# An embedding, attention and feed-forward stage: its first loads issued at once, and its weight preparation spread over VectorE's order

## The reference, cut to what matters

```python
h = concat([patches @ W + b, table[ids]], axis=1)            # 64 image tokens, 128 text tokens
x = layernorm(h)
scores = (x @ wq.T) @ (x @ wk.T).T / sqrt(256); attn = softmax(causal(scores))
h = h + attn @ (x @ wv.T)
alpha = mean(abs(w)); w_t = sign(w) * (abs(w) > 0.5 * alpha)  # for w_up and w_down
h = h + ternary(gelu(ternary(layernorm(h), w_up)), w_down)
# second layer: log_lam = -8 * softplus(omega) * sigmoid(xi @ Wl.T + bl), and so on
```

## Time and profile before

| | before |
|---|---|
| median of 3 runs | 1068.57 us (1068.31 to 1074.8) |
| profiled execution | 1078.99 us, its span 1077.2 us |
| TensorE (PE) busy in the span | 944.6 us, 88% |
| VectorE (DVE) | 827.7 us, 77% |
| ScalarE (ACT) | 571.5 us, 53% |
| GpSimd (POOL) | 544.5 us, 51% |
| mean granted TensorE clock | 0.947 |

### The profile page before, as it was taken

The page is one execution under the profiler, slowest core; times in us unless marked ns, Lnnn a source line. Parts: engine busy times, 40 slices in busy tenths (PEclk is TensorE's granted clock), DMA queues, the critical chain, the costliest instruction groups (busy, mean ns, idle before and its releaser), DMA issues. The chain is left out here.

```text
span 1077.2 us, 19311 instructions
## 1 busy us (share of the span) xinstructions
PE 944.6 (88%) x5800; PEld 840.2 (78%) x5800; DVE 827.7 (77%) x2441; ACT 571.5 (53%) x1127; POOL 544.5 (51%) x652
## 2 busy tenths in 40 slices
PE   2379999999999999876988999999999999962898
PEld 2269999999999999864567888888888888852787
DVE  2657888888888888764368889989999989874676
ACT  2136555555555555542546666667776667521342
POOL 2126666666666665443424444445555445433463
PEclk9589999999999999987989999999999999965999
DMA  4200311111111114002299999999999999983310
GB/s 140 65 25 26 40 41 40 39 40 44 41 45 39 41 44 156 16 15 73 31 121 130 145 154 150 147 159 153 156 153 151 147 152 137 134 99 102 106 59 20
DMA packets 134814, 96.32 MB, mean 89 GB/s; under 512 B 11208, under 2 KB 129104, under 8 KB 134096
## 3 DMA queue, kind: packets, MB, share of 16 engines
q1 hardware_dynamic: 133200, 91.20, 56.5%
q0 software_dynamic: 1536, 4.20, 1.3%
HBM read 31.92 MB, written 13.11 MB: 42 GB/s over the span
## 5 line engine op out<-in xcount | busy, mean ns | idle before, releaser
L296 POOL TENSOR_TENSOR gelu_lo<-gelu_out,gelu_hi 128x384 fp32r<-128x384 f32 x128 | 151.9, 1206 | 40.5 <-DVE gelu_hi L483 39.4
L893 POOL TENSOR_TENSOR B_decayed_u<-B_scan_in 128x512 f32<-128x512 f32 x48 | 62.0, 1293 | 102.9 <-DMA B_scan_in<-B_stage 92.0
L657 PE MATMUL psA<-ternary_down,gelu_hi 128*128 128x256 f32 x384 | 101.2, 299 | 10.8 <-POOL gelu_lo L296 10.8
L610 PE MATMUL psA<-x2T_hi,ternary_up 128*128 128x384 f32 x256 | 93.7, 366 | 10.6 <-DVE residual L590 10.5
L657 PE MATMUL psA<-ternary_down,gelu_lo 128*128 128x256 f32 x384 | 96.9, 288 | 0.0
L610 PE MATMUL psA<-x2T_lo,ternary_up 128*128 128x384 f32 x256 | 87.5, 342 | 0.0
L657 PEld LDWEIGHTS psA<-ternary_down,gelu_hi 128*128 128x128 f32 x384 | 74.4, 194 | 16.0 <-POOL gelu_lo L296 15.1
L1129 PE MATMUL psB<-Win_hi,B_x_hi 128*128 128x512 f32 x192 | 83.7, 436 | 0.0
L1141 PEld LDWEIGHTS psB<-B_partial_dots,B_minus_same_batch 128*128 128x128 f32 x384 | 66.7, 195 | 19.9 <-DVE B_partial_dots L1025 8.8
L881 POOL TENSOR_TENSOR B_y<-B_scan_in,B_states 128x512 f32<-128x512 f32 x48 | 61.9, 1290 | 38.4 <-ACT B_states L952 38.4
L1041 DVE SCALAR_TENSOR_TENSOR psB<-B_decayed_u,psB 128x128 f32<-128x128 f32 x192 | 68.0, 354 | 13.6 <-PE psB L1141 13.3
(11 more groups left out here) (247 smaller groups left out, 3350.6 us busy)
## 6 DMA issues: line engine op xcount, KB each, us to landing
B_scan_in<-B_stage SPq DMA_DIRECT2D x192, 256.0 KB, 8.3
patches<-in_patches SPq DMA_DIRECT2D x16, 384.0 KB
B_residual<-layer_out SPq DMA_DIRECT2D x48, 128.0 KB, 5.1
out_dram<-B_residual SPq DMA_DIRECT2D x48, 128.0 KB, 5.0
C_raw<-in_experts SPq DMA_DIRECT2D x8, 768.0 KB, 4.2
layer_out<-residual SPq DMA_DIRECT2D x32, 128.0 KB, 1.8
layer_out<-residual SPq DMA_DIRECT2D x32, 64.0 KB, 2.0
weight_stage<-in_upT SPq DMA_DIRECT2D x1, 1024.0 KB, 5.7
```

Of the source, the lines that this page charges most:

```text
L296: nc.gpsimd.tensor_tensor(act_l[:, k, :], act[:, k % DEEP, :], act_h[:, k, :].bitcast(F32), ALU.subtract).then_inc(s["ffn_lo"], 1)
L610: last = nc.tensor.matmul(out, a, b, start=(n == 0), stop=(n == len(terms) - 1))
L657: last = nc.tensor.matmul(ps[:, 6 + k // 2, (k % 2) * D:(k % 2 + 1) * D], x[:, c, k * P:(k + 1) * P], dn_w[:, c, :], start=(c == 0 and x i ...
L893: nc.gpsimd.tensor_tensor(lu[:, j % 2], ring[:, j % R_RING, :, LAM, :], ring[:, j % R_RING, :, U, :], ALU.mult).then_inc(s["lu"], 1)
```

## The change

All of it is in part A. `order` gets the pieces merge, qk_split, abs_up, abs_down, tern_up and tern_down, which do their work for tile 0 alone (offset 1 for those of down, so that they run in period -1, and 2 for the others, period -2); `ternary` and `chunk` 2 leave `prepare`. SyncE issues the loads of period -3 without waits: `weight_stage` holds the three chunks side by side, and the two ternary weights land in `W.raw_l` and `W.raw_v`. The ids and the gather of tile 0 move to period -4. VectorE casts the patches of tile 0 before it splits weights. The merge writes bank 4 and runs after `tok` of tile 0. `up` of tile 0 waits for the up weights alone, `down` for both. The load of the channel vectors moves to period 12, and the softplus and the store of its rows to period 15, where ScalarE loads the Gelu table again behind it.

```diff
+        MERGED = ps[:, 4, :].rearrange("p (a b) -> p a b", a=DC)
...
-        order = """ids_load exp gelu_table tok ternary.0 up.0 up.1 pT patch_split patch_load emb pT_split root1 gelu.0 gelu.1 v
-                v_split apply1 up.2 up.3 gelu.2 add.1 up.4 pv gelu.3 add.2 xT gelu.4 up.5 x_split ternary.1
-                gelu.5 up.6 add.3 up.7 gelu.6 gelu.7 exp_table t h1 root2 gather t_split add.4 add.5
+        order = """ids_load exp gelu_table tok merge up.0 up.1 pT patch_split patch_load emb pT_split root1 gelu.0 gelu.1 v
+                v_split apply1 qk_split abs_up abs_down up.2 up.3 gelu.2 add.1 up.4 pv gelu.3 add.2 xT gelu.4 up.5 x_split
+                gelu.5 up.6 add.3 up.7 gelu.6 gelu.7 exp_table t h1 root2 gather t_split tern_up tern_down add.4 add.5
                 down.0 down.1 score scale2 add.6 add.7 x2T down.2 max ss x2_split rscale
                 h2.0 h2.1 h2.2""".split()
         order = [(w.split(".")[0], int((w + ".0").split(".")[1])) for w in order]
         offset = {"up": 0, "gelu": 0, "add": 0, "down": 0, "ss": 0, "rscale": 0, "h2": 0, "tok": 2, "emb": 2, "root1": 2, "apply1": 2,
-                  "xT": 2, "x_split": 2, "t": 2, "t_split": 2, "score": 2, "max": 2, "ternary": 2, "patch_load": 4, "ids_load": 3,
+                  "xT": 2, "x_split": 2, "t": 2, "t_split": 2, "score": 2, "max": 2, "abs_up": 2, "abs_down": 1, "tern_up": 2, "tern_down": 1, "merge": 2, "qk_split": 2, "patch_load": 4, "ids_load": 3,
                   "patch_split": 3, "gather": 3}
...
-        chunks_of = {-3: (0, 1, 2)}
-        tern_of = {-2: (0, 1)}
+        chunks_of = {-3: (0, 1)}
...
+        stage_at = (0, 1024, 1536)
+        raw_tern = [W.raw_l[:].rearrange("p a b -> p (a b)"), W.raw_v[:].rearrange("p a b -> p (a b)")]
+        tern_in = [s["tern_in0"], s["tern_in1"]]
...
                 if g == -4:
+                    sp.dma_start(ids[:, 0, :], io["ids"][0]).then_inc(ids_in[0], 16)
+                if g == G - 4:
                     sp.dma_start(vec[:], io["vectors"]).then_inc(s["vec_in"], 16)
-                if g == 1:
+                if g == G - 1:
                     sp.wait_ge(s["c8"], 1)
                     sp.dma_start(W.rows[0].rearrange("(k m p) -> p k m", p=P, k=3), vec[:],
                                  allow_slow_non_contiguous=True).then_inc(s["rows_out"], 16)
                 if g == G - 4:
+                    sp.wait_ge(s["w_sum"], 4)
                     for a, b in ((W.raw_in, io["WinT"]), (W.raw_l, io["WlT"]), (W.raw_v, io["WvT"]), (W.raw_out, io["WoutT"])):
                         sp.dma_start(a[:].rearrange("p a b -> p (a b)"), b).then_inc(s["raw_in"], 16)
-                for n in chunks_of.get(g, ()):
-                    src, _, _, cols = chunks[n]
-                    if n >= 2:
-                        sp.wait_ge(s["w_lo"], n - 1)
-                    sp.dma_start(stage_half[n % 2][:, 0:cols], src).then_inc(stage_in[n % 2], 16)
                 if g == -3:
+                    def chunk(n):
+                        src, _, _, cols = chunks[n]
+                        sp.dma_start(stage[:, stage_at[n]:stage_at[n] + cols], src).then_inc(stage_in[n], 16)
+
+                    chunk(0)
+                    chunk(1)
                     sp.dma_start(wq, io["wq"]).then_inc(s["qk_in"], 16)
                     sp.dma_start(wk, io["wk"]).then_inc(s["qk_in"], 16)
                     sp.dma_start(bias_tok[:], io["tokb"]).then_inc(s["const_in"], 16)
-                for n in tern_of.get(g, ()):
-                    sp.wait_ge(s["w_lo"], 3)
-                    wait(sp, s["w_sum"], 2 * n)
-                    sp.dma_start(stage[:], tern[n][0]).then_inc(s["tern_in"], 16)
+                    chunk(2)
+                    for n in range(2):
+                        sp.dma_start(raw_tern[n], tern[n][0]).then_inc(tern_in[n], 16)
...
-                if kind == "ids_load":
+                if kind == "ids_load" and not (isinstance(n, int) and n == 0):
...
+            def gather(n, sl, half):
+                pool.wait_ge(ids_in[sl], 16 * (half + 1))
+                wait(pool, s["h1_done"], n - 1)
+                settle(pool)
+                for j in range(2):
+                    pool.indirect_dma_start(
+                        emb[:, sl, 1 + j, :], None, io["table"],
+                        bass.IndirectOffsetOnAxis(ap=ids[:, sl, j:j + 1], axis=0),
+                    ).then_inc(text_in[sl], 16)
+
+            def prepare(g):
+                if g == -4:
+                    gather(0, 0, 0)
+
...
-                if g == -2:
+                if g == G - 1:
                     sc.wait_ge(s["c1"], 1)
                     nc.scalar.activation(soft[:, 1, :], soft[:, 0, :], ACT.Exp, scale=-1.0).then_inc(s["c2"], 1)
                     sc.wait_ge(s["c3"], 1)
                     nc.scalar.activation(soft[:, 3, :], soft[:, 2, :], ACT.Ln).then_inc(s["c4"], 1)
+                    wait(sc, s["gelu_warmed"], G)
+                    nc.scalar.activation(warm_gelu[:], ones[:, 0:1], ACT.Gelu)
                 for n in chunks_of.get(g, ()):
-                    _, hi_, _, cols = chunks[n]
-                    sc.wait_ge(stage_in[n % 2], 16 * (n // 2 + 1))
-                    nc.scalar.activation(hi_, stage_half[n % 2][:, 0:cols], ACT.Copy).then_inc(s["w_hi"], 1)
-                if g == -3:
-                    sc.wait_ge(s["merge_ps"], 1)
-                    nc.scalar.activation(qk_h[:], SC[:, 0:DC * D].rearrange("p (a b) -> p a b", a=DC), ACT.Copy,
-                                         scale=float(D) ** -0.5).then_inc(s["qk_ready"], 1)
+                    chunk_hi(n)
+
+            def chunk_hi(n):
+                _, hi_, _, cols = chunks[n]
+                sc.wait_ge(stage_in[n], 16)
+                nc.scalar.activation(hi_, stage[:, stage_at[n]:stage_at[n] + cols], ACT.Copy).then_inc(s["w_hi"], 1)
...
+                if kind == "qk_split" and isinstance(n, int) and n == 0:
+                    sc.wait_ge(s["merge_ps"], 1)
+                    nc.scalar.activation(qk_h[:], MERGED, ACT.Copy, scale=float(D) ** -0.5).then_inc(s["qk_ready"], 1)
+                    chunk_hi(2)
...
-            def ternary(n):
-
-                out = tern[n][2]
-                v.wait_ge(s["tern_in"], 16 * (n + 1))
-                nc.vector.tensor_reduce(abparts[:], stage[:].rearrange("p (a b) -> p a b", a=32), AX_X, ALU.add,
+            def abs_sum(n):
+                raw = raw_tern[n]
+                v.wait_ge(tern_in[n], 16)
+                nc.vector.tensor_reduce(abparts[:], raw.rearrange("p (a b) -> p a b", a=32), AX_X, ALU.add,
                                         apply_absolute_value=True).then_inc(s["w_abs_parts"], 1)
                 v.wait_ge(s["w_abs_parts"], n + 1)
                 nc.vector.tensor_reduce(absum[:, n:n + 1], abparts[:], AX_X, ALU.add).then_inc(s["w_abs"], 1)
...
+                raw, out = raw_tern[n], tern[n][2]
...
             def prepare(g):
+                if g == G - 1:
+                    softplus()
+                if g == -3:
+                    patch_hi(0)
+                for n in chunks_of.get(g, ()):
+                    chunk_lo(n)
                 if g == -2:
-                    softplus()
-                for n in chunks_of.get(g, ()):
-                    _, hi_, lo_, cols = chunks[n]
-                    v.wait_ge(s["w_hi"], n + 1)
-                    nc.vector.tensor_tensor(lo_, stage_half[n % 2][:, 0:cols], hi_.bitcast(F32),
-                                            ALU.subtract).then_inc(s["w_lo"], 1)
-                if g == -3:
-                    v.wait_ge(s["qk_ready"], 1)
-                    nc.vector.scalar_tensor_tensor(out=qk_l[:], in0=SC[:, 0:DC * D].rearrange("p (a b) -> p a b", a=DC),
-                                                   scalar=float(D) ** -0.5, in1=qk_h[:].bitcast(F32), op0=ALU.mult,
-                                                   op1=ALU.subtract).then_inc(s["qk_ready"], 1)
                     v.wait_ge(s["const_in"], 16)
                     v.wait_ge(s["mask_ready"], 1)
+
+            def chunk_lo(n):
+                _, hi_, lo_, cols = chunks[n]
+                v.wait_ge(s["w_hi"], n + 1)
+                nc.vector.tensor_tensor(lo_, stage[:, stage_at[n]:stage_at[n] + cols], hi_.bitcast(F32),
+                                        ALU.subtract).then_inc(s["w_lo"], 1)
+
+            def patch_hi(n):
+                v.wait_ge(s["patch_in"], 16 * (n + 1))
+                wait(v, s["tok_done"], n)
+                nc.vector.tensor_copy(pat_h[:], patches[:]).then_inc(s["patch_hi"], 1)
...
+                if kind == "qk_split" and isinstance(n, int) and n == 0:
+                    v.wait_ge(s["qk_ready"], 1)
+                    nc.vector.scalar_tensor_tensor(out=qk_l[:], in0=MERGED, scalar=float(D) ** -0.5,
+                                                   in1=qk_h[:].bitcast(F32), op0=ALU.mult,
+                                                   op1=ALU.subtract).then_inc(s["qk_ready"], 1)
```

(30 more changed lines are left out.)

35 lines of the change are left out of this document (7 added, 28 removed).

## The result

The changed kernel takes 1065.61 us, median of 20 runs (1054.2 to 1069.39); the kernel before takes 1076.15, median of 20 (1068.31 to 1085.06). The ratio is 0.9907, 95% interval 0.9885 to 0.9929. The forecast was 1054.2 in 1048.5 to 1061, so the time lies above the range. Two things must be kept apart. The three runs of before that stood ahead of the prediction (median 1068.57; they are three of the 20) lay low in a spread of 17 us: over 20 runs the median is 7.6 us higher. And the shift itself is 1065.61 - 1076.15 = -10.5 us, not -14.4.

A forecast was written before the change was run, and what follows sets the result against it. TensorE was taken to bound the repeated periods, untouched; the head was to be bound by the second patches' landing at 16.9 us. Head -16.6 plus last period +2.2 gave -14.4, from 1068.57 to 1054.2 us, range 1048.5 to 1061.

The forecast's parts named there:

- Sum: Whole kernel: head -16.6 and last period +2.2 give -14.4 us, taken from the median of 1068.57 to 1054.2.
- Tile 0: Head, cast of second patches to row maxima: cast -18.0 us, `t` -19.5, maxima -19.0 after tern_up's +0.5.
- Tile 0, next period: Head, to up.0: abs_down costs nothing, tern_down delays x_normed 3.9 us, up.0 +2.4, so first period starts -16.6 us.
- I take 390: Head, early loads: 3.67 MB left after 7.4 us move at 390 GB/s in 9.4 us, patches 1 landing at 16.9.
- I give 0 in the sum, and 2 us either way in the range: Head, TensorE's clock: half-clock stretches fall otherwise; 18 `tok` matmuls take 1.9 us at full, 3.8 at half clock.
- Last period: Last tile: softplus before gelu.0, with two table loads, delays it by +2.2 us; bounds 1.6 to 3.9.
- A port, weighed: Head, tern_down beside GpSimd's gather issue: an issue holds VectorE back by next to nothing, despite the skill's shared-port rule.
- (c): Rival, head: shared port makes tern_down wait for both gather issues, +2.1 us, 1056.3; chance 0.10.
- (b): Rival, head: loads at 299 GB/s put the cast at 19.7, +2.8, half-clock `tok` +1.7: 1058.7 us; chance 0.17.
- (a): Rival, head: second patches not held back by the queue, cast at 13, 3.9 us more gain, 1050.3; chance 0.12.
- (d): Rival, repeated periods: head hands over a lasting half clock, about 24 us per whole period, 1078, slower; chance 0.03.
- (e): Rival, head: early loads bring nothing; about 4 us gained against 2.4 and 2.2 of delays, 1068; chance 0.03.

The follow-up runs named there:

- e1: Changed kernel with both 1 MB ternary loads issued behind the patches of tile 1 instead of ahead; 0.9833 of the kernel before.
- e7: Changed kernel with the gather of tile 0 back in its old place, period -3; 0.9899 of the kernel before.
- e3: Changed kernel with tern_up ahead of `t`, abs_down behind t_split, tern_down at the head of the next period; 0.981 of before, second run 1057.95 us.
- e5: Changed kernel with the edits of e1, e2 and e3 together, run twice; 0.9822 and 0.9853 of the kernel before.
- e6: Changed kernel with the edits of e1, e2 and e3 and the filler matmuls of e4; 0.9843 of the kernel before.
- e2: Changed kernel with the softplus, its load and its store back in the head and the Gelu reload gone; 0.9816 of the kernel before.
- f1: Changed kernel with unread matmuls, 12 behind the scores of tile 1 and 8 behind x2T of tile 0; 1064.88 us, single run.
- e4: Changed kernel with filler matmuls that nobody reads in seven places of the head; 0.9873 of the kernel before.

## Why the prediction was wrong

**The base, "Sum".** "The median is 1068.57 ... a shift holds for it: 1054.2" is the step that failed most. I had seen that the profiled execution (1078.99) and the median of three runs lay 1% apart, and took the three for the kernel's time. Over 20 runs it is 1076.15. The mean of the three runs shown differs from it by 5.6 us; with the profiled execution as a fourth sample the spread of 10.7 us was in plain view, and the range should have held half of it on the upper side. With the forecast's own shift and the base of 20 runs the number would have been 1061.8, still 3.9 us below 1065.61; with the means of all runs it is 1060.5 against 1063.0. (The 1064.6 that the forecast names for the profiled execution lies 1 us from the median by luck: its base was 2.8 us too high and its shift 3.9 too large.)

**The shift, "Tile 0" and "Tile 0, next period".** Step by step, forecast against the mean of three profiles of each kernel:

- Cast of the second patches: -18.0, measured -17.05 (18.0 instead of 16.9). The mechanism, the queue that holds a small late load, was right (e1, e7), and so was "I take 390": by 7.4 us the three profiles had moved 1.19 to 1.23 MB (1.18 in the forecast), and from there to 16.5 they ran at 389, 400 and 400 GB/s. The term that was mis-sized is the last one, "so patches 1 land when all 4.85 MB are through": it has the cast follow the bulk of the bytes at once. The first profile (the last column is GB/s):

```profile
7.40:16.50 9.10, 4.71 (x23) 4.63 (x24) 1.83 (x2) 1.58 (x2) 1.66 (x1) 1.00 0.99 389
16.50:18.00 1.50, 0.97 (x5) 0.52 (x3) 0.00 (x0) 0.49 (x1) 0.00 (x0) 1.00 0.17 57
18.00:18.58 0.58, 0.00 (x0) 0.00 (x0) 0.00 (x0) 0.58 (x2) 0.00 (x0) 1.00 0.00 0
```

  The last bytes trickle for 1.5 us, and VectorE starts 0.6 us after the last of them. In the repeats the trickle is 0.4 and 0.9 us, and the start again 0.5 to 0.6 us behind it. The cast so stood 1.0 to 2.1 us behind 16.5.
- Cast to row maxima of tile 0: -1.0, measured -1.26. Its parts came out: xT_lo is held by qk_lo, wv_lo and the sum, 1.1 us (forecast 1.3); `t` no longer waits for a ternary matmul; and from tT_lo to neg_max it takes 6.31 us with tern_up, in all three profiles, 0.5 more than the mean before (6.07, 6.53 and 4.75), as forecast.
- tern_down: "denominators and x_normed end 3.9 us later". ln_den follows tT_lo after 5.16 us instead of 0.87 to 1.45, and the maxima of tile 1 come 2.3 us later.
- Then "`tok` takes 2.2 us more, until about 84.4" and, of the clock, "**I give 0 in the sum, and 2 us either way in the range**": this is the step of the shift that failed. In all seven profiles with tern_down ahead of x_normed and no filler in the pause (1.7 to 3.4 us), `tok` of tile 2 ran at half clock for half of its time or more, and up.0 came 3.2 to 4.2 us after the maxima. In all eight without tern_down there (three of before, e3 twice, e5 twice, e6) it came 2.33 to 2.34 us after them. The mean of three of after is 3.82, +1.5 us. That was no chance to be put in the range but a consequence of the pause: before, x2T follows the scores of tile 1 without one; now TensorE first waits 1.7 to 2.5 us for x_normed.
- Together -14.4 at up.0 (67.64 instead of 82.01) against -16.6 forecast. What differs from profile to profile is the clock elsewhere: from the maxima of tile 0 to tT_lo of tile 1 the first profile of after took 19.11 us, with `tok` and `t` of tile 1 at half clock, its repeats 16.15 and 16.35. That is most of what sets its up.0 (70.15) apart from theirs (66.42 and 66.35).

**"Last period".** +2.2, measured +2.27 on the stretch and +1.96 at gelu.0 in the means of three; e2 takes it away. Right in size, place and make-up: two tables of 1.28 us and three short instructions. Together with the head the shift by the profiles is -12.1 us, and by the means of all runs -11.9; the 20 runs beside 20 say -10.5. Of part A as a whole the profiles show -11.2: the repeated periods took 0.9 us more in the mean, inside the 394.8 to 397.9 us that they took in the 16 profiles.

**Covers given as nothing** held: abs_down, the moved ids and the rows' store, the softplus's absence in the head (e2).

**"A port, weighed".** The bound held for VectorE: tern_down's steps took 0.75 and 1.28 us beside the gather's issue, as without it. Next to nothing is not nothing, though: in e2 a step that began inside an issue took 0.87 instead of 0.75, and the x_normed of the earlier trace rows, which did too, 1.25 where it takes 1.06 clear of one (changed kernel, 64.19). In the changed kernel's first profile it was the issue that became longer, where it began inside one of those steps (59.69 to 60.44). GpSimd:

```profile
58.39 1.11 POOL L293 DMA_INDIRECT embedded<-in_table,text_ids  x1 [0.19 <-issue]
59.80 1.47 POOL L293 DMA_INDIRECT embedded<-in_table,text_ids  x1 [0.30 <-issue]
```

1.47 us instead of 0.96, and 1.48 at the same place in e7, with nobody waiting for it. The Trainium skill (SBUF — State Buffer, "Who interferes with whom") says that issue order decides which of the two engines waits for a shared port; these cases agree in the direction (the one that came second took longer), and rival (c), which had VectorE wait, did not come about.

**Rivals.** (b), late loads and the clock, was the nearest: both of its parts came, at 1.1 and 1.5 us instead of 2.8 and 1.7, the first not by its reason, a rate of 299 GB/s, but by the end of the loads. (a) is refuted by e1 and e7, (d) and (e) by the table of stretches.

## What to carry to other kernels

A step that moves work into another engine's pause on the way to TensorE costs its own delay and, where it opens a pause on TensorE (here 1.7 to 2.5 us), the clock of what follows: here the next 18 matmuls ran at half clock for half or more of their time in seven of seven profiles. Price the next matmuls so from the start, and look first for a pause that nothing of TensorE hangs on (e3). Loads issued at once from one queue were served in their order here: put the small one that the chain needs ahead of the megabytes that it doesn't (e1), and put a table switch where an engine idles, not ahead of the last tile (e2). And before a shift of 1% is added to a median of three, look at how far the three and the profiled execution are apart: here that was as much as the effect.

## What the runs showed of the hardware

- The half clock depends on what TensorE did before, and more than the last pause counts. At the same place the scores of tile 1 took 3.21, 3.61 and 3.95 us in the three profiles of the changed kernel, and 2.42, 3.24 and 3.47 in those of the kernel before, where 2.42 is full clock throughout; `tok` behind them ran at 1.00 from start to end only where TensorE had not paused ahead of x2T, or hardly (before, e3, e5, e6 and f1). In front of `t` of tile 0 shortening a pause from 2.94 to 0.80 us brought nothing (e4: 4.21 us), while with the earlier cast and the same fillers (e6) `t` took 3.08. Why the one and not the other stays open. Behind that `t`, with fillers in the pauses, eight of eight groups of matmuls ran at full clock (e4 and e6), without them 19 of 56.
- From 4 to 9 us the loads ran at 309 to 341 GB/s in the three profiles of the changed kernel, from 9 to 16 at 414 to 416. That the size of the loads sets this is not shown: the 256 KB of wk and wv landed inside the second stretch. The first 512 KB of tokW landed 5.8, 4.3 and 5.2 us after their issue in these three: part of this is chance.
- The load of the second patches ended with a trickle of 0.4 to 1.5 us at 24 to 57 GB/s, and VectorE, which waited for it, started another 0.5 to 0.6 us later.
- Parts B and C, untouched by every edit, took 563.7 to 572.2 us in 16 profiled executions: 8 us of chance, as much as the best version gains over the changed kernel.
